# Attention block of a graph network on one core: x in a second, transposed layout, split on GpSimd

## What is computed

```python
q = heads(x @ Wq); k = heads(x @ Wk); v = heads(x @ Wv)      # x: (64, 128, 256)
scores = jnp.einsum('bhnd,bhmd->bhnm', q, k) / sqrt_dk
scores = jnp.where(mask, scores, -jnp.inf)
attn = jax.nn.softmax(scores, axis=-1)
out = jnp.einsum('bhnm,bhmd->bhnd', attn, v)                 # then (b, n, d)
x = _layernorm(x + jax.nn.relu(out) @ Wo)
x = _layernorm(x + gnn(x, adj, ...))                         # three layers
```

## Time and profile before

| | |
|---|---|
| median of three runs | 1895.2 us |
| profiled execution: span | 1892.0 us |
| what lies around the span, to the median | 3.2 us |
| TensorE busy, whole span | 1672.9 us (88%) |
| VectorE busy | 1513.0 us (80%) |
| GpSimd busy | 1314.4 us (69%) |
| ScalarE busy | 1120.7 us (59%) |

### The profile page before, as it was taken

The page is one execution under the profiler, slowest core; times in us unless marked ns, Lnnn a source line. Parts: engine busy times, 40 slices in busy tenths (PEclk is TensorE's granted clock), DMA queues, the critical chain, the costliest instruction groups (busy, mean ns, idle before and its releaser), DMA issues.

```text
span 1892.0 us, 40139 instructions
## 1 busy us (share of the span) xinstructions
PE 1672.9 (88%) x12032; PEld 1482.6 (78%) x12032; DVE 1513.0 (80%) x5366; ACT 1120.7 (59%) x2718; POOL 1314.4 (69%) x1690
## 2 busy tenths in 40 slices
PE   5999999965999999999899999999989898989895
PEld 4777777754888888888788888888878787878784
DVE  3888888877788778788887887887888888888873
ACT  3888888864556556556465565565554545554542
POOL 3355555534787787787777877877868787888786
PEclk8999999996999999999899999999999898999998
DMA  5233333323121121121211211211212122212101
GB/s 181 63 89 89 89 89 89 89 79 123 34 67 58 42 67 58 42 67 54 91 56 44 67 52 47 67 53 47 67 34 68 64 70 65 68 64 69 63 26 45
DMA packets 150477, 127.31 MB, mean 67 GB/s; under 512 B 14880, under 2 KB 143392, under 8 KB 150432
## 3 DMA queue, kind: packets, MB, share of 16 engines
q1 hardware_dynamic: 145024, 124.30, 21.4%
q10 hardware_dynamic: 5408, 2.50, 0.5%
HBM read 89.03 MB, written 37.75 MB: 67 GB/s over the span
## 4 chain that ended last, share of the span: by engine, by line
PE 24%; DVE 20%; POOL 19%; issue 11%; ACT 3%; POOLq 1%; DVEq 0%; ACTq 0%
PE ps L45 14%; PE ps L819 6%; POOL gnn_norm L154 5%; DVE gnn_junk L913 5%; PE ps L795 3%; DVE gnn_small L929 2%; POOL gnn_norm L742 2%; POOL gnn_h L746 2%; POOL xo L761 2%; POOL gnn_norm L757 2%; POOL inv L149 2%; DVE gnn_small L934 2%; DVE gnn_small L937 2%; DVE gnn_res L972 1%; DVE gnn_st L976 1%
## 5 line engine op out<-in xcount | busy, mean ns | idle before, releaser
L819 PE MATMUL ps<-gnn_w_hi,gnn_g_hi 128*128 128x256 f32 x1536 | 454.8, 296 | 41.7 <-DVE gnn_res L972 41.0
L819 PE MATMUL ps<-gnn_w_lo,gnn_g_hi 128*128 128x256 f32 x1536 | 445.7, 290 | 0.0
L819 PE MATMUL ps<-gnn_w_hi,gnn_g_lo 128*128 128x256 f32 x1536 | 444.9, 290 | 0.0
L141 POOL TENSOR_TENSOR fence_pool<-half_neg 128x1 f32<-128x1 f32 x304 | 64.1, 213 | 477.3 <-DVE gnn_mv L1063 169.0
L980 DVE TENSOR_TENSOR gnn_g_lo<-ps,gnn_g_hi 128x512 fp32r<-128x512 f32 x384 | 263.1, 685 | 135.3 <-ACT ps L893 135.2
L892 ACT ACTIVATE gnn_g_hi<-ps,b_cols 128x512 fp32r<-128x512 f32 x384 | 264.5, 689 | 179.4 <-PE ps L45 155.3
L819 PEld LDWEIGHTS ps<-gnn_w_hi,gnn_g_hi 128*128 128x128 f32 x1536 | 305.6, 199 | 47.5 <-DVE gnn_res L972 44.8
L45 PE MATMUL ps<-gnn_hT_hi,gnn_w_hi 128*128 128x512 f32 x768 | 333.4, 434 | 4.0 <-DVE gnn_g_lo L980 4.0
L869 ACT ACTIVATE gnn_e<-gnn_u,gnn_small 128x128 f32<-128x128 f32 x192 | 74.9, 390 | 400.3 <-DVE gnn_small L938 400.3
L819 PEld LDWEIGHTS ps<-gnn_w_lo,gnn_g_hi 128*128 128x128 f32 x1536 | 306.7, 200 | 1.9
L819 PEld LDWEIGHTS ps<-gnn_w_hi,gnn_g_lo 128*128 128x128 f32 x1536 | 305.8, 199 | 0.0
(11 more groups left out here) (116 smaller groups left out, 3925.2 us busy)
## 6 DMA issues: line engine op xcount, KB each, us to landing
hist<-xo SPq DMA_DIRECT2D x48, 512.0 KB, 3.3
x<-hist SPq DMA_DIRECT2D x48, 512.0 KB, 4.3
gmask<-mask_hist SPq DMA_DIRECT2D x48, 256.0 KB, 4.5
aw<-in_L_gnn_attn_w SPq DMA_DIRECT2D x48, 256.0 KB, 4.3
att_xq<-in_x SPq DMA_DIRECT2D x16, 512.0 KB, 4.8
att_xl<-in_x SPq DMA_DIRECT2D x16, 512.0 KB, 3.5
gnn_fin<-hist SPq DMA_DIRECT2D x16, 512.0 KB, 3.8
out<-gnn_fin SPq DMA_DIRECT2D x16, 512.0 KB, 2.8
```

Of the source, the lines that this page charges most:

```text
L141: e.tensor_tensor(fence_pool[:, n:n + 1], half_neg[:, 0:1], half_neg[:, 0:1], ALU.add)
L819: mm = e.matmul(FF2[j % 2], g[a][:, m, j * N:(j + 1) * N], V[b][:, m, :], start=(n == 0), stop=(n == len(terms) - 1))
```

## The change

The host passes x a second time as `xT`, laid out as step, feature within the half, half, graph, node: 16 x 128 x 1024. SyncE loads a step of it into `xT_raw` by one DMA of 4 KB a partition. GpSimd makes both parts out of it in `split_xT`: one copy of 128x1024 to the high part, one subtraction of 128x1024 to the low part. It does so after the masks of the step in hand, when all six projections that read the old `xT` are done (`proj_made`). TensorE's `transpose_x`, ScalarE's `xT_hi` and VectorE's `xT_lo` go; the buffer `xq` goes. The next load into `xT_raw` waits for the split of the one before (`xT_lo_out`). The residual still uses x in the old layout (`xl`).

```diff
@@ -235,22 +235,26 @@
                     e.dma_start(xl[par][:], block_of(x_g, t)).then_inc(x_ld[par], 16)
                     e.dma_start(adjl[par][:], block_of(adj_g, t)).then_inc(x_ld[par], 16)
 
+                def load_xT(t):
+                    e.dma_start(xT_raw[:].rearrange("p k n -> p (k n)"),
+                                xT_in[bass.ds(t, 1)].rearrange("o p n -> p (o n)")).then_inc(xT_ld, 16)
+
                 for sem in stored + mask1_st:
                     e.sem_inc(sem, START)
-                e.dma_start(xq[:], block_of(x_g, 0)).then_inc(xq_ld, 16)
+                load_xT(0)
                 for n, w in ((0, Wq), (1, Wk)):
                     e.dma_start(w_raw[:, n], w.rearrange("(k p) n -> p k n", p=P)).then_inc(wa_ld[0], 16)
                 load(0, 0)
                 load(1, 1)
-                e.wait_ge(xT_made, 2)
-                e.dma_start(xq[:], block_of(x_g, 1)).then_inc(xq_ld, 16)
+                e.wait_ge(xT_lo_out, 1)
+                load_xT(1)
                 load_layer_weights(e, 0)
 
                 def body(q, par, more):
                     t = 2 * q + par
                     if more:
-                        e.wait_ge(xT_made, 2 * (t + 2))
-                        e.dma_start(xq[:], block_of(x_g, t + 2)).then_inc(xq_ld, 16)
+                        e.wait_ge(xT_lo_out, t + 2)
+                        load_xT(t + 2)
 
                     e.wait_ge(masks_made, 2 * (t + 1))
                     e.dma_start(block_of(mask_hist, t), mask1[par][:]).then_inc(mask1_st[par], 16)
@@ -297,7 +301,18 @@
                     hold_pool(e, mask1_st[par], START + 16 * q1)
                     e.tensor_scalar(mask1[par][:], eye_sum[:], 0.0, MASKED, ALU.is_le, ALU.mult).then_inc(masks_made, 1)
 
+                def split_xT(t1):
+
+                    hold_pool(e, xT_ld, 16 * (t1 + 1))
+                    if not isinstance(t1, int) or t1:
+                        hold_pool(e, proj_made, 6 * t1)
+                    e.tensor_copy(xT[0][:], xT_raw[:]).then_inc(xT_hi_out, 1)
+                    e.wait_ge(xT_hi_out, t1 + 1)
+                    e.tensor_tensor(xT[1][:], xT_raw[:], xT[0][:].bitcast(F32), ALU.subtract).then_inc(xT_lo_out, 1)
+
+                split_xT(0)
                 make_masks(0, 0, 0)
+                split_xT(1)
 
                 e.wait_ge(const_ld, 16 * (5 + L))
                 e.tensor_tensor(affine[:, :, 2, :], affine[:, :, 1, :], b2_rows[:], ALU.add).then_inc(aff_set, 1)
@@ -308,6 +323,8 @@
                         e.wait_ge(masks_made, 2 * (t + 1))
                         e.wait_ge(peaked, GROUP * t + 1)
                         make_masks(q + (par + 1) // 2, 1 - par, t + 1)
+                    if a2:
+                        split_xT(t + 2)
                     if isinstance(t, int) and t == NG - 1:
                         return
                     e.wait_ge(stored[par], START + 16 * q)
@@ -319,23 +336,12 @@
             def _(e):
                 e.wait_ge(ident_set, 1)
 
-                def transpose_x(t1, k):
-
-                    if k == 0:
-                        e.wait_ge(xq_ld, 16 * (t1 + 1))
-                    if not isinstance(t1, int) or t1:
-                        e.wait_ge(proj_out, 6 * t1 - 1 + k)
-                    for j in range(GROUP):
-                        mm = e.transpose(A[k][:, j * N:(j + 1) * N], xq[:, j, k * P:(k + 1) * P], ident[:])
-                    mm.then_inc(xT_made, 1)
-
                 def project(t1, par, n, parts=(0, 1)):
 
                     bank = A[n % 2]
                     if n == 0 and 0 in parts:
-                        e.wait_ge(xT_hi_out, 2 * (t1 + 1))
-                        e.wait_ge(xT_lo_out, 2 * (t1 + 1))
-                    if n >= 2 and 0 in parts:
+                        e.wait_ge(xT_lo_out, t1 + 1)
+                    if 0 in parts and (n >= 2 or not isinstance(t1, int) or t1):
                         e.wait_ge(proj_out, 6 * t1 + n - 1)
                     if n < 4:
                         mm = split_product(e, bank, (w_hi, w_lo), xT,
@@ -362,9 +368,6 @@
 
                     if j < 3 and a1:
                         project(t + 1, 1 - par, 2 * j + half, parts)
-                    if j == 3 and half == 0 and a2:
-                        for k in parts:
-                            transpose_x(t + 2, k)
 
                 def body(q, par, a1, a2):
                     t = 2 * q + par
@@ -404,14 +407,10 @@
                         split_product(e, PB[0][:, 0:D], attT, (w_hi, w_lo), lambda x, k: x[:, k, :],
                                       lambda w, k: w[:, 3, k, :]).then_inc(wo_made, 1)
 
-                for k in range(KT):
-                    transpose_x(0, k)
                 for n in range(6):
                     e.wait_ge(wa_split, 2 if n < 4 else 4)
                     project(0, 0, n)
                 scores(0, 0, 0)
-                for k in range(KT):
-                    transpose_x(1, k)
                 e.wait_ge(scored, 1)
                 scores(1, 0, 1)
                 steps(e, body)
...
@@ -451,9 +446,6 @@
                             proj_copy(t + 1, 1 - par, 2 * (j - 1) + 1)
                         e.wait_ge(pT_made, 2 * i + 1)
                         e.copy(probsT[:, 4:8, :].rearrange("p h n -> p (h n)"), PB[1]).then_inc(pT_out_b, 1)
-                        if j == 3 and a2:
-                            for k in range(KT):
-                                xT_hi(t + 2, k)
                         if has1 and j < 3:
                             e.wait_ge(peaked, i + 2)
                             exps(i + 1, (j + 1) % 2, 0)
@@ -465,9 +457,6 @@
                                 exps(i + 1, (j + 1) % 2, 0)
                             exps(i + 1, (j + 1) % 2, 1)
 
-                for k in range(KT):
-                    xT_hi(0, k)
-
                 for n, c in ((0, g1), (1, beta1), (3, g2), (4, beta2)):
                     e.dma_start(affine[:, :, n, :], on_all(c)).then_inc(const_ld, 16)
                 e.dma_start(b2_rows[:], on_all(b2)).then_inc(const_ld, 16)
@@ -476,8 +465,6 @@
                         e.dma_start(b1_cols[:, l, :], b1[l].rearrange("(m p) -> p m", p=P)).then_inc(const_ld, 16)
                 for n in range(6):
                     proj_copy(0, 0, n)
-                for k in range(KT):
-                    xT_hi(1, k)
                 e.wait_ge(peaked, 1)
                 exps(0, 0, 0)
                 exps(0, 0, 1)
...
@@ -542,8 +524,6 @@
                         e.tensor_copy(probsT[:, 0:4, :].rearrange("p h n -> p (h n)"), PB[0]).then_inc(pT_out_a, 1)
                         if j == 0 and before:
                             statistics(i - 1, 1 - par, GROUP - 1)
-                        if j == 3 and a2:
-                            xT_lo(t + 2)
 
                         e.wait_ge(rdenT_out, START + i + 1)
                         e.wait_ge(pv_made, i + 1)
...
@@ -1104,8 +1082,14 @@
              "L1_gnn_W1", "L1_gnn_b1", "L1_gnn_W2", "L1_gnn_b2", "L1_gnn_g1", "L1_gnn_beta1", "L1_gnn_g2",
              "L1_gnn_beta2"]
     arrays, args = {}, []
+    x = np.asarray(inputs["x"])
+    B, N, D = x.shape
+    laid = dict(inputs)
+    laid["xT"] = (x.reshape(B // GROUP, GROUP, N, D // P, P).transpose(0, 4, 3, 1, 2)
+                  .reshape(B // GROUP, P, D // P * GROUP * N))
+    names.insert(1, "xT")
     for name in names:
-        a = np.ascontiguousarray(inputs[name])
+        a = np.ascontiguousarray(laid[name])
         arrays[f"in_{name}"] = a
         args.append(nc.dram_tensor(f"in_{name}", a.shape, mybir.dt.from_np(a.dtype), kind="ExternalInput").ap())
     out = nc.dram_tensor("out", arrays["in_x"].shape, F32, kind="ExternalOutput").ap()
```

More of the change, by code:

```diff
@@ L47, in split_product, with gnn_kernel @@
     return last
-def gnn_kernel(nc, x_in, adj, Wq, Wk, Wv, Wo, attn_w, attn_b, W1, b1, W2, b2, g1, beta1, g2, beta2, out):
+def gnn_kernel(nc, x_in, xT_in, adj, Wq, Wk, Wv, Wo, attn_w, attn_b, W1, b1, W2, b2, g1, beta1, g2, beta2, out):
     B, N, D = x_in.shape
@@ L169, in gnn_kernel @@
             w_lo = sb("w_lo", [P, 4, KT, D], F32R)
-            xq = sb("xq", [P, GROUP, D])
+            xT_raw = sb("xT_raw", [P, KT, TOK])
             xl = [sb(f"xl{i}", [P, GROUP, D]) for i in range(2)]
@@ L194, in gnn_kernel @@
             wa_ld = sems("wqk_ld", "wvo_ld")
-            wa_split, xq_ld = sems("wa_split", "xq_ld")
+            wa_split, xT_ld = sems("wa_split", "xT_ld")
             x_ld = sems("x_ld_even", "x_ld_odd")
-            (masks_made, xT_made, xT_hi_out, xT_lo_out, proj_made, proj_out, s_made, scored, peaked, exped,
+            (masks_made, xT_hi_out, xT_lo_out, proj_made, proj_out, s_made, scored, peaked, exped,
              pT_made, pT_out_b, pT_out_a, pv_made, den_inv, rden_out, rdenT_made, rdenT_out, att_out,
              attT_hi_out, attT_lo_out, wo_made, y_out, bn_out, eye_made, eye_added) = sems(
-                "masks_made", "xT_made", "xT_hi_out", "xT_lo_out", "proj_made", "proj_out", "s_made", "scored",
```

(10 more changed lines are left out.)

## The result

The changed kernel takes 1940.24 us, median of four runs (1937.81 to 1940.84); the kernel before, run beside it, 1894.84 us. The ratio is 1.0238 (95% interval 1.0223 to 1.0252): 2.4% slower, and 6 us from the forecast of 1934. Its profiled span is 1938.5 us, 46.5 more than before; the execution that was profiled took 1940.53 us, so 2.0 us lie around its span.

A forecast was written before the change was run, and what follows sets the result against it. VectorE's chain in graph 3 of each attention step was taken to set the pace. 1892.0 - 2.2 (start) + 35 (waits) + 6 (clock) = 1930.8 us of span, with 3.2 around it: forecast 1934 us, range 1900 to 1956.

The forecast's parts named there:

- Bound: In graph 3, the last of an attention step's four, VectorE's chain sets the pace; TensorE waits 1.10 us.
- L539 waits to 228.6: In graph 3, VectorE's spread of the reciprocals, ready at 226.6, waits for GpSimd's subtraction and ends about 228.7, not 226.02.
- VectorE operations that read and write only SBUF wait out a GpSimd instruction: Port rule read from profile rows: such VectorE work stands until the running GpSimd instruction ends.
- The two-input form does: Port rule narrowed: not all GpSimd work blocks VectorE, but its two-input operations do.
- Removal: Taking the split of x off TensorE, ScalarE and VectorE gains 0.21 us a step, not 1.28.
- The copy: GpSimd's 128x1024 copy in graph 3: 1.6 us, between 1.1 and 3.0, from about 224.3 to 225.9.
- The net: Per attention step: 2.7 us of lateness on VectorE's chain, +2.5 after 0.21 saved; fourteen steps, +35 us.
- The subtraction: GpSimd's two-input operation of 128x1024 in graph 3: 2.40 us, up to 3.9 if the rounded output costs more.
- rival 3: Rounded format slow on GpSimd: subtraction 3.9 us, 1.5 more a step, +21, total 1955 us; chance 0.14.
- The clock: TensorE idle over 3 us in graph 3 drops to half clock: 1.2 us in five of fourteen steps, +6 (0 to 24).
- The one example of the second block: After TensorE idled 2.7 us there, the next but one stretch ran at 0.51, 1.2 GHz of 2.4.
- Start: At kernel start: constants' DMAs issued earlier, -4.3 us; second split blocks VectorE, +2.1; together -2.2.

The follow-up runs named there:

- experiment 3: Changed kernel with a second GpSimd copy of 128x1024 in place of the subtraction from the third block on: 1894.50 us, ratio 1.0009.
- experiment 4: Changed kernel with GpSimd's subtraction cut into two, four or eight instructions: 1901.22, 1887.74 and 1895.02 us.
- experiment 5: Changed kernel with sixteen unused transposes of raw weights on TensorE during its wait in graph 3: 1910.77 us, ratio 1.0091.
- experiment 6: Changed kernel with the reciprocals written to PSUM, so that VectorE's spread reads PSUM: 1891.65 us, ratio 0.9995.
- experiment 9: Changed kernel with the subtraction in four instructions and the constants' DMAs issued by SyncE behind the first layer's weights: 1881.53 us, ratio 0.9942.
- experiment 1: Changed kernel without GpSimd's copy and subtraction from step 2 on: 1886.74 us, ratio 0.9960.
- experiment 7: Kernel before, nothing removed, with a copy and a subtraction of 128x1024 on scratch buffers added on GpSimd: 1933.30 us, ratio 1.0215.

## Why the prediction was right, and where it was not

The direction, the mechanism and its place held; two sizes in the sum were wrong and balanced each other.

- **Bound.** Graph 3's chain on VectorE sets the pace: shown by experiments 3, 4 and 5. Over its undisturbed 0.29 us the spread grew by 0.16, 0.33, 0.70 and 1.79 us (four pieces, second copy, two pieces, whole subtraction with TensorE busy), and the step over its 23.65 by 0.15, 0.33, 0.65 and 1.79, as long as the clock held.
- **The port.** "L539 waits to 228.6": shown. The spread ends with the subtraction, waits for a one-input copy too, and doesn't wait when it reads PSUM. Of the Trainium skill, page "SBUF — State Buffer", section "SBUF: two separate sides", the exclusive lock for a whole instruction agrees with this (2.06 us with one instruction, 0.99 with two, 0.45 with four). One reading of mine was too wide and one too narrow. "VectorE operations that read and write only SBUF wait out a GpSimd instruction" is too wide: L507 and L519 don't. "The two-input form does" is too narrow: the one-input copy holds the spread as well. L555, which L298 left alone in the kernel before, stays unexplained: it was not tried which part of that GpSimd compare makes the difference.
- **Removal.** I took 0.21 us a step; 0.35 was measured: 5 us in fourteen steps instead of 3.
- **The copy: the step that failed first.** I took 1.6 us from a layernorm row with start costs; it takes 1.04, just below the 1.1 that was my lower bound. The page "GPSIMD Engine Reference" of the Trainium skill, section "Elementwise — side-by-side cycle accounting", gave an estimate of 0.9 us; that was nearer than my 1.6. With 1.04 the copy ends 0.17 us after `neg_peak` begins (which lasts 0.20 us, not about 1), the subtraction starts earlier by as much, and the spread waits 1.77 us longer than it takes undisturbed, where I had 2.7 from both. The net is +1.4 us a step, not +2.5: 20 us in fourteen steps, not 35.
- **The subtraction** cost 2.34 us for 2.40 taken; the rounded output is no dearer, so rival 3 falls.
- **The clock: the step that failed second.** I expected a pause of over 3 us, a drop in five of fourteen steps and 1.2 us each, +6. The pause is 2.03, the clock falls in every step that splits, and this costs 1.9 us: 14 x 1.9 = 26 us, outside my 0 to 24. Two sizes were off: the number of falls, 14 and not 5, and the length of one, 6.8 us and not 3.4. For a stretch of 3.4 us the 1.2 was about right (0.9 to 1.3 in the single falls of experiments 3, 4, 6 and 9). The one example of the second block could give neither.
- **Start.** Taken -4.3 and +2.1; measured -4.2 at TensorE's restart and -3.6 at the first exponential, behind a wait of about 0.9 us for the second split (L502 takes 1.01 for 0.17). Against it, the statistics of the first step come 1.5 us later than before, 5.1 lost within it. From the first exponential to these statistics it is 28.8 us before, 29.9 without the two instructions (experiment 1), 31.8 with TensorE kept busy (experiment 5) and 34.0 in the change. So 4.1 of the 5.1 are the wait and the clock fall of this step's own split, and 1.1 are there without them; experiment 1 has the second split and a stretch at the lower clock from 30 to 38 us as well.

The balance of the span: -3.6 at the start, +5.1 in the first step, and the 13 steps behind it, 3.46 more each on average (the longer first one, 28.5, is among them), +45.0; together the 46.5 that were found. By cause it is about 25 us of waits, 26 of clock, 5 less by the removal and 3.6 less at the start, with some 4 left, nearly all in the first two steps. My sum had 35 net for waits and 6 for the clock. The direction was right by the mechanism; that 1934 came so near was luck, because 15 too many stood against 20 too few.

One slip in the working cost nothing: the 0.69 us from L520 to L539 run from start to start, and I added them to the end of L520, so L539 would have been ready at about 226.4 and not 226.6; it waits for the subtraction either way.

## What to carry to other kernels

Before work goes to GpSimd "because it idles", list VectorE's SBUF-to-SBUF instructions that will run beside it and ask which of them TensorE waits for; the price is the rest of the GpSimd instruction, so its length per instruction counts and not the total. Cut it into pieces, or let the urgent copy read PSUM: either took the whole loss away here. And in a loop of like steps a new pause of TensorE can cost its length in every step and, if the clock falls behind it, more: here 1.8 and 1.9 us.

## What was not expected of the hardware

- A pause of 2.03 us behind dense work was followed by 6.8 us at 0.52 of the full clock, in all fourteen steps that split; keeping TensorE at work through the same wait with transposes that nobody reads made the kernel 29.5 us faster.
- Pauses of 1.53 and 1.10 us lowered the clock in eight of fourteen steps (experiment 7). Single falls of 3.4 us came even where the largest pause in a step was 0.84 us (experiment 9). What decides stays open.
- VectorE's statistics of 128x256 and its reciprocal of 128x8, both on SBUF only, ran beside GpSimd's subtraction in 0.43 and 0.18 us, while the 128x256 copy from SBUF to SBUF waited for its end.
- Each further GpSimd instruction cost 0.15 to 0.2 us: 1, 2, 4 and 8 instructions for the same 128x1024 took 2.34, 2.55, 2.84 and 3.52 us.
- Three issues of the b1 columns held ScalarE's queue for 13.51 us from 5.69 on, among the first large loads; the same three took SyncE 6.43 us from 18.16 on.
